# Macaron block (MoE FFN, attention, MoE FFN) on one core: routing with roots on GpSimd and top eight taken from exponentials, expert weights issued behind the routing's stores

## What is computed

```python
def moe(x):                                    # E=64 experts, K=8, F=96, at most C=64 tokens an expert
    probs = softmax(x @ router_w.T)            # T x 64
    topk_w, topk_ids = top_k(probs, 8)
    topk_w = topk_w / sum(topk_w)
    # every expert takes its first 64 tokens in token order, the rest are dropped
    y = (silu(xb @ w_gate) * (xb @ w_up)) @ w_down          # per expert
    routed = segment_sum(y[slot] * topk_w, token)
    shared = (silu(sg) * su) @ ws_down                      # sg, su = halves of x @ ws_gate_up
    return routed + shared

x = x + 0.5 * moe(layernorm(x))
x = x + attn(layernorm(x))                     # 16 heads of 8, softmax, projection, residual, layernorm with gamma, beta
x = x + 0.5 * moe(layernorm(x))
```

## Time and profile before

| | before |
|---|---|
| median of 3 runs | 964.06 us (962.13 to 964.1) |
| profiled execution | 963.40 us, its span 961.6 |
| PE, DVE, ACT, POOL busy | 702.0, 635.7, 462.6, 384.7 us |
| DMA | 80.18 MB, mean 83 GB/s |
| granted TensorE clock, mean | 0.817 of full speed |
| chain that ended last | PE 47%, DVE 18%, DMA 9%, ACT 8%, issue 8%, POOL 5% |

### The profile page before, as it was taken

One profiled execution on the slowest core, in us unless ns is written; L12 is line 12 of the kernel. 1 busy time (PEld: TensorE's weight loads), 2 busy tenths in 40 slices (PEclk: granted clock), 3 DMA queues, 4 the chain that ended last, 5 costly groups with the idle time before them and its releaser, 6 DMA issues.

```text
span 961.6 us, 16608 instructions
## 1 busy us (share of the span) xinstructions
PE 702.0 (73%) x4710; PEld 354.3 (37%) x4771; DVE 635.7 (66%) x1570; ACT 462.6 (48%) x1007; POOL 384.7 (40%) x480
## 2 busy tenths in 40 slices
PE   0256658783169999999999999999960459388870
PEld 0244347572113333333333333333210444377660
DVE  3289824433478888888888888888817699424430
ACT  0223323331015777777777777777765234133330
POOL 1152657865741333223332233321005426658852
PEclk9999856855558999999999999999995559556755
DMA  8941243332443454444444444445110122523324
GB/s 239 250 107 53 80 143 44 53 39 22 101 92 67 81 94 91 96 88 93 80 89 95 88 93 80 89 95 90 33 46 3 56 71 60 165 37 50 53 25 101
DMA packets 219782, 80.18 MB, mean 83 GB/s; under 512 B 149880, under 2 KB 213528, under 8 KB 219672
## 3 DMA queue, kind: packets, MB, share of 16 engines
q1 hardware_dynamic: 197160, 59.70, 28.7%
q0 software_dynamic: 12288, 10.49, 7.4%
q10 hardware_dynamic: 10288, 9.44, 3.9%
HBM read 49.94 MB, written 31.49 MB: 85 GB/s over the span
## 4 chain that ended last, share of the span: by engine, by line
PE 47%; DVE 18%; DMA 9%; ACT 8%; issue 8%; POOL 5%; ACTq 3%; DVEq 0%; POOLq 0%; SPq 0%
PE psum L1294 13%; PE psum L1285 11%; PE psum L1272 10%; DMA sums<-sums_sb,sidx 6%; PE psum L1208 5%; ACT arena L1067 4%; POOL sums L580 3%; ACTq L965 2%; DVE arena L744 2%; DVE arena L742 2%; PE psum L1181 2%; ACT arena L1014 2%; DVE arena L862 2%; DMA arena<-dispatch_rows,arena 1%; DVE arena L706 1%
## 5 line engine op out<-in xcount | busy, mean ns | idle before, releaser
L862 DVE TENSOR_REDUCE arena<-psum 128x2 f32<-128x1024 f32 x256 | 309.1, 1221 | 51.8 <-PE psum L1272 48.3
L1067 ACT ACTIVATE arena<-psum 128x512 f32<-128x512 f32 x512 | 282.1, 600 | 115.1 <-PE psum L1285 105.1
L1272 PE MATMUL psum<-arena 126*128 126x512 bf16 x512 | 199.8, 397 | 8.7 <-DVE arena L862 4.1
L1285 PE MATMUL psum<-arena 128*128 128x512 bf16 x451 | 173.2, 387 | 7.1 <-ACT arena L1067 3.3
L1294 PE MATMUL psum<-arena 128*32 128x512 f32 x1024 | 136.2, 604 | 1.3 <-ACT arena L1058 1.3
L580 POOL DMA_INDIRECT sums<-sums_sb,sidx x64 | 102.0, 1593 | 62.9 <-DVE sums_sb L810 33.7
L628 POOL CAST arena<-arena 128x256 bf16<-128x256 f32 x32 | 12.7, 396 | 267.5 <-issue 263.5
L1285 PEld LDWEIGHTS psum<-arena 128*128 128x128 bf16 x512 | 50.6, 100 | 150.1 <-ACT arena L1067 122.6
L810 DVE COPY sums_sb<-psum 128x256 f32<-128x256 f32 x32 | 13.6, 424 | 115.9 <-DMA sums<-sums_sb,sidx 65.8
L563 POOL DMA_INDIRECT arena<-dispatch_rows,arena x64 | 62.8, 981 | 26.0 <-issue 13.4
L1014 ACT ACTIVATE arena<-psum,arena 64x128 f32<-64x128 f32 x128 | 46.3, 362 | 45.3 <-PE psum L1181 42.9
(11 more groups left out here) (137 smaller groups left out, 1106.0 us busy)
## 6 DMA issues: line engine op xcount, KB each, us to landing
arena<-qk_parts SPq DMA_DIRECT2D x128, 96.0 KB
ctx<-arena SPq DMA_DIRECT2D x32, 256.0 KB, 2.0
qk_parts<-arena SPq DMA_DIRECT2D x32, 192.0 KB, 3.7
dispatch_rows<-xn_sb SPq DMA_DIRECT2D x16, 256.0 KB, 2.3
sums<-x_sb SPq DMA_DIRECT2D x16, 256.0 KB, 2.3
arena<-lists SPq DMA_DIRECT2D x8, 512.0 KB, 5.7
arena<-qk_parts SPq DMA_DIRECT2D x64, 64.0 KB
arena<-ctx SPq DMA_DIRECT2D x64, 64.0 KB, 2.3
```

The source lines that it names most:

```text
L862: dve.tensor_reduce(mx_r[r % 2][:, 2 * p:2 * p + 2], src, X, ALU.max).then_inc(a_mx, 1)
L1067: act.activation(p_r[tau % NPB], bank[4 + tau % 2][:, :], ACT.Exp, scale=SCALE).then_inc(a_P, 1)
L1272: ins = pe.matmul(bank[tau % 4][:, :], heads(q_st[r], rows, g)[:, qt * P:(qt + 1) * P], heads(k_st[r], rows, g), start=True, stop=True)
L1285: pe.matmul(bank[4 + tau % 2][:, :], keys, heads(q_st[r], rows, g), start=True, stop=True)\
```

## The change

In the routing, in both FFNs:

- the reciprocal root is taken on POOL as a power of -0.5, four tiles at a time, right ahead of the group's normalisation; ACT's Sqrt and DVE's reciprocal of it go (also in attention's two layernorms);
- DVE takes the negated row maximum, ACT four exponentials a group straight from the logits in PSUM with that as bias; DVE finds the top eight among the exponentials, marks them with 2.0, writes the mask, and sums the eight values; the subtraction, the masking of the exponentials and the 64-wide sum go;
- POOL makes the weights in two products, of group g-2 ahead of normalising group g; PE does the logits of group g-1 behind the transposes of group g; ACT likewise.

In the first FFN the statistics of a group are taken by DVE one group at a time between the routing steps, and at the end of attention also the means and variances by group. SP issues the expert weights in 24 pieces of eight experts behind the last store of the routing, and the attention loads behind those. The lists come back in eight DMAs of 256 KB instead of four, of which the later ones wait for PE's transposes.

```diff
             def ffn(f):                                   # SP
...
-                store(0, 0)
-                store(1, 1)
-                store_w(0, 0)
-                with sp.Fori(1, NG // 2) as i:
...
+                if f.p == 0:
+                    for g in range(NG):
+                        store(g, g % 2)
+                        if g:
+                            store_w(g - 1, (g - 1) % 2)
+                    store_w(NG - 1, 1)
+                    for c in range(24):
+                        expert_weights(c)
+                    attention_weights()
...
-                for c in range(NQ // 4):
-                    part = slice(c * 4 * 2 * P, (c + 1) * 4 * 2 * P)
+                for c in range(NQ // 2):
+                    part = slice(c * 4 * P, (c + 1) * 4 * P)
+                    wait(sp, f.gtp, 2 * c - 3 if c > 1 else c)
...
                 def normalise(g, r):                      # POOL
+                    wait(pool, f.aggr, GT * g + GT)
+                    rs = rstd[:, bass.ds(g * GT, GT)]
+                    pool.tensor_scalar(rs, mv[:, bass.ds(g * GT, GT), 1], LN_EPS, None, ALU.add).then_inc(f.ve.sem, 1)
+                    wait(pool, f.ve, g + 1)
+                    pool.tensor_tensor(rs, rs, power[:, 0:GT], ALU.pow).then_inc(f.rs.sem, 1)
...
+                def weights(g, r):
+                    wait(pool, f.ws[r], 16 * ((g - r) // 2) if isinstance(g, int) else 8 * (g - r))
+                    wait(pool, f.key, g + 1)
...
+                    pool.tensor_tensor(w, e_r[r].rearrange("p (j e) -> p j e", j=GT), kk, ALU.mult).then_inc(f.es.sem, 1)
+                    wait(pool, f.es, g + 1)
+                    wait(pool, f.rden, g + 1)
+                    pool.tensor_tensor(w, w, den_r[r].unsqueeze(2).to_broadcast([P, GT, E]), ALU.mult).then_inc(f.w.sem, 1)
...
+                for g in range(2, NG):
+                    weights(g - 2, g % 2)
+                    normalise(g, g % 2)
+                weights(NG - 2, 0)
+                weights(NG - 1, 1)
...
-                    dve.tensor_reduce(m_r[r], lg, X, ALU.max).then_inc(f.mx.sem, 1)          # DVE
+                    dve.tensor_reduce(m_r[r], lg, X, ALU.max, negate=True).then_inc(f.mx.sem, 1)
...
+                        dve.max(top[:, j, :], e[:, j, :]).then_inc(f.top.sem, 1)
...
+                        dve.match_replace(d[:, j, :], top[:, j, :], e[:, j, :], 2.0).then_inc(f.rep.sem, 1)
+                    dve.tensor_reduce(den_r[r], top, X, ALU.add).then_inc(f.den.sem, 1)
+                    dve.tensor_scalar(kk[:, bass.ds(g * GT, GT), :], d, 1.5, None, ALU.is_gt).then_inc(f.key.sem, 1)
+                    dve.tensor_scalar(den_r[r], den_r[r], 2.0, None, ALU.mult).then_inc(f.den2.sem, 1)
...
-            for w, t in ((w_gate, wg_sb), (w_up, wu_sb), (w_down, wd_sb)):                   # ACT
-                act.dma_start(t[:], w.rearrange("e k n -> k e n")).then_inc(s_wexp, 16)
...
+                    for j in range(GT):
+                        ins = act.activation(e_r[r][:, j * E:(j + 1) * E], bank[2 + r][:, j * E:(j + 1) * E], ACT.Exp,
+                                             bias=m_r[r][:, j:j + 1])
...
+                transposes(0, 0)                                                             # PE
+                if f.p == 0:
+                    pe.wait_ge(s_rws, 1)
+                transposes(1, 1)
+                logits(0, 0)
                 with pe.Fori(1, NG // 2) as i:
                     for r in range(2):
-                        route(2 * i + r, r)
+                        transposes(2 * i + r, r)
+                        logits(2 * i + (r - 1), 1 - r)
+                logits(NG - 1, 1)
...
-                pe.wait_ge(s_wexp, 48)
+                pe.wait_ge(s_wexp, 16 * 24)
```

More of the change, by code:

```diff
@@ L607, in center @@
                 xt = x_sb[:, bass.ds(t, 1), :].rearrange("p a d -> p (a d)")
-                wait(pool, a_rs, 1 if isinstance(t, int) else 0)
+                if isinstance(t, int) and t in (0, GT):
+                    last = GT if t == 0 else NT
+                    pool.wait_ge(a_aggr, last)
+                    pool.tensor_scalar(rstd[:, t:last], mv[:, t:last, 1], LN_EPS, None, ALU.add).then_inc(a_ve, 1)
+                    pool.wait_ge(a_ve, 1 if t == 0 else 2)
+                    pool.tensor_tensor(rstd[:, t:last], rstd[:, t:last], power[:, t:last], ALU.pow).then_inc(a_rs, 1)
+                    pool.wait_ge(a_rs, 1 if t == 0 else 2)
                 wait(pool, a_use, use("x", t - 2) + 1 if not isinstance(t, int) or t >= 2 else 0)
@@ L646, in attention @@
                         prep(NBUF * i + r, r)
+                pool.wait_ge(a_za, NT)
+                pool.tensor_scalar(rstdz[:], mvz[:, :, 1], LN_EPS, None, ALU.add).then_inc(a_zve, 1)
+                pool.wait_ge(a_zve, 1)
+                pool.tensor_tensor(rstdz[:], rstdz[:], power[:], ALU.pow).then_inc(a_zrs, 1)
                 for g in range(NG):
@@ L709, in route @@
-                    dve.scalar_tensor_tensor(out=e_r[r], in0=d_r[r], scalar=0.5, in1=e_r[r],
-                                             op0=ALU.is_gt, op1=ALU.mult).then_inc(f.es.sem, 1)
-                    wait(dve, f.es, g + 1)
-                    dve.tensor_reduce(den_r[r], e, X, ALU.add).then_inc(f.den.sem, 1)
+                        wait_apart(dve, (f.top, g * GT + j + 1))
+                        dve.match_replace(d[:, j, :], top[:, j, :], e[:, j, :], 2.0).then_inc(f.rep.sem, 1)
+                    wait(dve, f.w, g - 1)
@@ L725, in ffn @@
[L725 to L727 removed]
+                dve.wait_ge(s_cst, 4)
+                if f.p == 0:
+                    for g in range(NG):
+                        if g % 2 == 0:
+                            dve.wait_ge(s_x[g // 2], 16)
+                        token_stats(f, g)
+                        if g == 1:
+                            dve.wait_ge(s_rwp, 1)
+                            dve.tensor_copy(rwT[:], bank[7][:, 0:E]).then_inc(s_rws, 1)
+                        if g > 1:
+                            route(g - 2, g % 2)
+                    route(NG - 2, 0)
+                    route(NG - 1, 1)
+                else:
+                    route(0, 0)
+                    route(1, 1)
+                    with dve.Fori(1, NG // 2) as i:
+                        for r in range(2):
+                            route(2 * i + r, r)
@@ L1029, in attention @@
             def attention():
-                def std(first, last, count):
-                    act.wait_ge(a_ve, count)
-                    act.activation(rstd[:, first:last], rstd[:, first:last], ACT.Sqrt).then_inc(a_sd, 1)
-                std(0, GT, 1)
                 def xT_copy(t, r):
@@ L1110, in route, with logits @@
                     ins.then_inc(f.xtp.sem, 1)
+                def logits(g, r):
                     wait(pe, f.xts, 2 * g + 1)
-                    wait(pe, f.d, GT * (g - 1))
+                    wait(pe, f.ex, g - 1)
                     for j in range(GT):
```

172 lines of the change are left out of this document (70 added, 102 removed).

## The result

| | before | after |
|---|---|---|
| median (4 runs each, side by side) | 963.1 us (961.61 to 964.1) | 1027.46 us (1025.35 to 1028.8) |
| ratio | | 1.0668 (95%: 1.0642 to 1.0693) |
| profiled execution, span | 963.40, 961.6 | 1027.87, 1025.9 |
| PE, DVE, ACT, POOL busy | 702.0, 635.7, 462.6, 384.7 | 704.8, 599.1, 465.3, 438.1 |

What follows compares the result with a forecast made beforehand. The prediction took routing as bound by VectorE before the change and by serial rounds after it, with late bases in the first FFN. Its sum: 963.4 + 30.2 + 34.8 = 1028.4, forecast 1028 us, range 1002 to 1056.

Steps and rivals of the forecast that it cites:

- The ring: Routing, both FFNs: the new order on GpSimd and PE makes groups serial, one at a time, 11.65 us a round.
- break-even of 6.2 us a group: Routing: the kernel gets faster only with rounds under 6.2 us; the rival with overlapping groups, 938 us, had chance 0.05.
- The length of a round: Routing: one serial round through GpSimd, PE, ACT and VectorE takes 11.65 us, bounds 10.7 and 12.9.
- weights: Term of a round: two products of 128x256 on GpSimd, with a wait, 1.45 us.
- Normalise: Term of a round on GpSimd: addition, power, subtraction to multiplication and a hop, 2.65 us, the power taken as 0.25.
- PE: Term of a round: start of transposes, the transposes, and logits until VectorE's start, 3.35 us.
- The rest: Term of a round: row maximum, exponentials, four maxima, replacements, sum of the top eight, comparison and hops, 4.2 us.
- First FFN: Last key at 93.7, weights on SP delay the bases, first gather at 152 instead of 119.30: +30.2 us in all.
- Rival 1: First FFN: weights on SP hardly delay the bases, first gather at 129.1, +7.3 us, time 1005.5; chance 0.13.
- The middle: Attention and final norm: roots leave ACT and VectorE for GpSimd, 0, within 1 us either way.
- Second FFN: Routing's last key at 830.1 against 792.77, +37.3 us, less 2.5 at the gathers: +34.8 us.
- Rival 2: Power on GpSimd far dearer than any row: at 3 us, 44 us more, about 1072; chance 0.07.

Runs made afterwards that it cites:

- experiments 1: Kernel after with normalise(g) moved ahead of weights(g-2) on GpSimd: 968.61 us, ratio 1.0002.
- 2: Kernel after with PE and ACT back to the logits and exponentials of the same group behind its transposes: 975.46 us, ratio 1.0063.
- 3: Kernel after with PE's order alone put back, ACT's left as changed: 1022.85 us, ratio 1.0549.
- experiment 6: Kernel after with three pieces of expert weights behind each store of normalised tokens, instead of all behind the last: 1006.45 us, ratio 1.045.
- Experiment 7: Kernel after with the root of attention's last layernorm back on ACT (Sqrt) and VectorE (reciprocal): 1021.48 us, ratio 1.0599.
- experiment 10: Kernel after with VectorE's routing of the second FFN written out for eight groups instead of a loop: 1033.47 us, ratio 1.0669.
- experiment 5: Kernel after with the addition and power of group g issued ahead of weights(g-2) on GpSimd: 1008.69 us, ratio 1.0462.
- first and third set: Two of the three sets of follow-up runs, each beside runs of the kernel before, whose medians there were 969.28 and 969.15 us.
- experiment 8: Kernel after with the 13 attention loads back at the start of SP's program: 1033.25 us, ratio 1.0658.
- second set: Another of the three sets of follow-up runs, beside runs of the kernel before, whose median there was 963.88 us.
- Experiment 4: Kernel before with the expert weights moved from ACT's queue to SP in 24 pieces behind the routing's last store: 954.56 us, ratio 0.9854.

## Why the prediction was right, point by point

**The ring.** Right, and shown from both sides (experiments 1 and 2 free it, 3 does not). Its break-even of 6.2 us a group, under which the change gains, is not shown by the times as they stand: 5.6 and 5.9 us only bring the time level with the kernel before (1.0002). It fits if the estimate holds that the stall weighs some 8 us against the run there. And the prediction named the order on GpSimd and PE and passed over ACT's, which closes the ring as well.

**The length of a round.** 11.65 were predicted, 11.1 and 11.8 came. Term by term, of the round shown above: weights 1.33 for 1.45. Normalise 3.5 for 2.65: the power was the term mis-sized, 1.04 us where 0.25 had been taken from the nearest row, VectorE's reciprocal at 0.18, and above the upper bound of 0.94. PE 2.87 for 3.35, since the logits start 0.2 us before the transposes are through, with their inputs copied a group ago, and take 1.84 to VectorE's start for 2.11. The rest 3.4 for 4.2: the four exponentials take 0.93 in all, where 1.4 were taken from twice as wide ones: each takes 0.31, and they overlap. The errors are +0.85 and -1.4: the sum was better than its terms.

**First FFN.** +30.2 predicted, +20.6 measured, the largest miss. Keys came at 90.0, not 93.7, by shorter rounds and a last group of 3.4 instead of 4.4. The routing's last stores were through at 91.9 and not at 95. The queue was sized nearly right: 32.4 us held against 36, with 275 GB/s moved in that window where 250 had been taken. The attention loads took 8.3 for 10.8, and the bases were 10 us as taken. So the gather was at 142.9 and not at 152, the sum of many small excesses in one direction. At the gathers 3.4 us came back for 2.5. Rival 1, that the bases are not late, fell to the 22.24 us of GpSimd's wait and to experiment 6.

The Trainium skill ("DMA: Bandwidth & Descriptors", section "Issuing engines are not separate DMA queues") calls the time that a sequencer takes to initiate a DMA usually small relative to the DMA itself. The trace leaves room for that with a single piece: 1.35 us on SP on the mean, with the DMA engines full, against a median of 4.9 to 7.1 to landing. What the rival overlooked is their sum, since 24 pieces in a row hold up what stands behind them for 32.4 us.

**The middle.** 0, within 1, was predicted; +5.7 came. The step that failed is "roots leave ACT and VectorE for GpSimd: 0". It priced a power of 128x32 as free work on an idle engine, but it stands on the path, and the power's time grows with the elements: 1.04, 4.82, 5.46 us for 4, 28, 32 a partition, some 0.16 for each. Experiment 7 gives 5.3 of the 5.7 back.

**Second FFN.** +34.8 predicted, +38.0 measured. Routing was +38.9 (65.2 - 26.3) for 37.3. Of that, 1.4 arose ahead of the first keys: the two first normalisations took 7.9 us (769.60 to 777.49) for 5.3, with the power dearer than taken in both, and the first addition and subtraction at 0.76 and 1.47 us for the later 0.23 and 1.04. The six rounds took 70.4 for 69.9, and that they agree is luck: the forecast priced a round too high, and VectorE's loop, which nothing in it had, made up for that. With the loop written out they take 67.0 (experiment 10), as in the first FFN (67.2). At the gathers 2.9 came back (65.2 to 62.3) for 2.5, and 2.0 were lost again in the expert steps.

**The sum.** +65.0 was predicted and +64.3 came in the span, by terms of which one was 9.6 too high, one 5.7 and one 3.2 too low. The total is right to 0.1%, and that is luck of the signs: with the first of these alone set right the forecast would have been 1019, with the two others alone 1037, both inside the range of 1002 to 1056. Rival 2, a power of 3 us, didn't come, though its sign did: the power costs 16.6 us of GpSimd's time in the routings, and with its addition 16.0 us of the twelve rounds (experiment 5), where the sum had 12 times 0.40.

## What to carry to other kernels

Before moving one step ahead of another on two engines, walk round from a group's result back to itself and count how many groups the ring carries: each "next group first" on one engine and "last group first" on another takes one away, and a ring with one group costs the sum of all engines' work in it, and what one of them sheds gains only if it lies in the ring. A transfer that nobody needs yet still holds the queue that issues it; put large loads between the stores of a stage whose queue is idle, and what the next stage waits for ahead of them. And price an operation that no row shows at its upper bound or above wherever it stands in a ring or alone on the path (here 1.04 us came where the bound was 0.94), and per element as well as per instruction.

## What was not expected of the hardware

- GpSimd's power costs by the element, some 0.16 us for each of a partition: 128x4 in 1.04 us, 128x32 in 5.46, where ACT's root and VectorE's reciprocal of 128x32 take 0.23 and 0.35.
- VectorE's routing in a loop, with waits on a register's value, made a round 0.6 us longer (11.8 to 11.2) than the same instructions written out (experiment 10), though each instruction's own length is the same; the gaps between them differ.
- PE's granted clock was at 1.00 (2.4 GHz) in the first routing and at 0.50 (1.2 GHz) in the second, by the two stretches above. PE's busy time for the same work, 18.28 and 18.29 us, and in experiment 10 the round, 11.2 us, did not show the difference.
- On the chips of the first and third set ACT stood still in the first expert steps of each FFN, for 8.15 us and 2.5 more in the first FFN of experiment 8, ended by what the trace calls another core or an unknown queue. In the second set and in the two profiles of the result nothing of the kind appears; the kernel before has no profile on the two chips. Experiment 4, built on the kernel before, has it too, though less: from the first gather to the first scatter 30.1 and 28.8 us, where the kernel before has 25.8 and 25.6. What queue it is stays open.
